# A transformer block on one core: the experts' second product in three terms, high parts of the weights by ScalarE

## The reference

```
x = layernorm(x + attention(x))                 # softmax attention, biases in all four products
xf = x.reshape(4096, 512)
ew, ei = top_k(xf @ gate_w.T, 2);  ew = softmax(ew)
expert e: (silu(xf @ w_gate[e].T) * (xf @ w_up[e].T)) @ w_down[e].T
routed = sum of the two chosen experts, each by its weight ew
shared = (silu(xf @ sh_gate.T) * (xf @ sh_up.T)) @ sh_down.T
out = layernorm(x + routed + sigmoid(xf @ se_gate_w.T) * shared)
```

## Time and profile before

| what | value |
|---|---|
| median, lowest, highest of the runs | 2044.42, 2044.05, 2047.7 us |
| the profiled execution: its own time, its span | 2047.9, 2046.2 us |
| mean granted TensorE clock | 0.989 |
| share of the chain that ended last | PE 86%, DVE 4%, DMA 3%, SPq 3%, issue 2% |
| store of the second product's result, 256 KB, issue to landing | 2.3 us, 71 of them |
| store of a high part, 256 KB | 2.4 us, 32 of them |
| load of an expert's high parts, 1 MB | 7.2 us, 8 of them |
| load of an expert's second weights, 512 KB | 20.8 us, 8 of them |

### The profile page before, as it was taken

The page is one execution under the profiler, slowest core; times in us unless marked ns, Lnnn a source line. Parts: engine busy times, 40 slices in busy tenths (PEclk is TensorE's granted clock), DMA queues, the critical chain, the costliest instruction groups (busy, mean ns, idle before and its releaser), DMA issues.

```text
span 2046.2 us, 31314 instructions
## 1 busy us (share of the span) xinstructions
PE 1971.2 (96%) x10048; PEld 1280.0 (63%) x10049; DVE 1344.6 (66%) x2296; ACT 888.2 (43%) x1571; POOL 942.9 (46%) x893
## 2 busy tenths in 40 slices
PE   7999999999999999999999998879999999999997
PEld 5655555755555755555755545568766666667886
DVE  5777776678777677777477776579233444446865
ACT  2366664366665366665266565311111111112322
POOL 3255654455665455665355556549111111114651
PEclk9999999999999999999999999989999999999999
DMA  7312433403432503432503323775643332347752
GB/s 231 73 41 70 99 79 93 140 23 85 102 79 71 162 17 82 99 92 54 170 27 69 68 74 104 260 303 181 249 170 103 102 97 98 103 168 228 224 174 71
DMA packets 103699, 242.11 MB, mean 118 GB/s; under 512 B 25296, under 2 KB 25808, under 8 KB 98576
## 3 DMA queue, kind: packets, MB, share of 16 engines
q1 hardware_dynamic: 92768, 205.06, 33.1%
q0 software_dynamic: 10800, 35.40, 6.2%
HBM read 132.93 MB, written 56.61 MB: 93 GB/s over the span
## 4 chain that ended last, share of the span: by engine, by line
PE 86%; DVE 4%; DMA 3%; SPq 3%; issue 2%; ACT 1%; POOL 1%; ACTq 0%; DVEq 0%; POOLq 0%
PE ps_gu L1698 18%; PE ps_s L723 11%; PE ps_side L701 11%; PE ps_ctx L734 10%; PE ps_side L675 9%; PE ps_d L1804 6%; PE ps_sum L747 5%; PE ps_d L1698 4%; PE ps_t L1769 1%; SPq L359 1%; PE ps_side L667 1%; DMA inv_rows<-inv_few 1%; DMA x_r<-x 1%; PE ps_side L772 1%; PE ps_side L769 1%
## 5 line engine op out<-in xcount | busy, mean ns | idle before, releaser
L1002 DVE TENSOR_REDUCE max_half<-ps_side 128x1 f32<-128x512 f32 x1024 | 658.8, 682 | 211.7 <-PE ps_side L701 208.5
L701 PE MATMUL ps_side<-kq_stack 96*128 96x512 f32 x1024 | 409.3, 404 | 4.9 <-DVE max_half L1002 2.3
L723 PE MATMUL ps_s<-kq_stack 97*128 97x512 f32 x937 | 392.2, 419 | 8.3 <-ACT probs_first L887 4.6
L723 PEld LDWEIGHTS ps_s<-kq_stack 97*128 97x128 f32 x937 | 177.4, 189 | 165.4 <-issue 85.5
L887 ACT ACTIVATE probs_first<-ps_s 128x512 f32<-128x512 f32 x326 | 187.7, 600 | 101.1 <-PE ps_s L723 85.5
L701 PEld LDWEIGHTS ps_side<-kq_stack 96*128 96x128 f32 x1024 | 195.5, 191 | 57.0 <-DVE max_half L1002 25.5
L887 ACT ACTIVATE probs_mid<-ps_s 128x512 f32<-128x512 f32 x308 | 177.5, 599 | 111.9 <-PE ps_s L723 97.3
L622 POOL TENSOR_TENSOR acc<-probs_first,probs_mid 128x512 f32<-128x512 f32 x129 | 163.8, 1296 | 131.1 <-ACT probs_mid L887 131.1
L887 ACT ACTIVATE probs_last<-ps_s 128x512 f32<-128x512 f32 x303 | 175.8, 599 | 99.2 <-PE ps_s L723 83.2
L622 POOL TENSOR_TENSOR acc<-probs_last,probs_first 128x512 f32<-128x512 f32 x129 | 163.3, 1292 | 117.6 <-ACT probs_first L887 117.6
L1653 POOL DMA_INDIRECT x_g<-x,who_all x71 | 67.4, 949 | 323.4 <-PE ps_t L1769 315.5
(11 more groups left out here) (252 smaller groups left out, 3674.2 us busy)
## 6 DMA issues: line engine op xcount, KB each, us to landing
kq_stack<-kq SPq DMA_DIRECT2D x192, 256.0 KB, 5.1
y_slots<-y_t SPq DMA_DIRECT2D x71, 256.0 KB, 2.3
x_r<-x SPq DMA_DIRECT2D x32, 256.0 KB, 3.9
x_t<-x SPq DMA_DIRECT2D x32, 256.0 KB, 4.1
gu_sb<-wgu SPq DMA_DIRECT2D x8, 1024.0 KB, 15.4
gu_kept<-gu_part SPq DMA_DIRECT2D x32, 256.0 KB, 2.4
gu_hi<-gu_kept SPq DMA_DIRECT2D x8, 1024.0 KB, 7.2
out<-gu_sb SPq DMA_DIRECT2D x32, 256.0 KB, 2.8
```

The source lines that it names most:

```text
L701: nc.tensor.matmul(bank, q_stack[par][0:3 * HD, h, t * P:(t + 1) * P], k_stack[par][0:3 * HD, h, half * HALF:(half + 1) * HALF], start=Tru ...
L723: nc.tensor.matmul(out, k_stack[par][0:3 * HD + 1, h, kt * P:(kt + 1) * P], q_stack[par][0:3 * HD + 1, h, half * HALF:(half + 1) * HALF], ...
L1002: nc.vector.reduce_max(max_half[:, u // 2, u % 2:u % 2 + 1], bank, AX.X).then_inc(side_free, 1)
```

## The change

- Attention: of the last batch's last group, the row sums of six pairs of steps (those that end no tile of keys) are issued one step later, after the second slot of scores.
- Scores: high and low router weights stand side by side (`rw_parts`), so a chunk of x takes two matmuls in place of three; what turns the scores back adds the two halves with a matrix `twice`. The first shared tile is turned and cut ahead of the last group's score (`FirstTile`).
- The high parts of the weights are made by ScalarE (`weights_high`) between its copies for the shared tiles: three parts in tile 1, five in tiles 2 to 10 each. There are now 48 parts, because the second product's weights are cut as well; their low parts (`wd_lo`) take the place of `wd_sb`, their high parts go to DRAM (`wd_kept`). GpSimd makes the low parts only, and gathers x for the first four expert tiles after part 40.
- The routing table: `positions` becomes `positions` (after tile 2) and `places` (after tile 3); all that follows comes one tile later.
- The first load of high parts is asked for when half of tile 11's product is done (`half_up`). The loads of x for shared tiles 14 and 15 move behind the expert tiles.
- Experts: x of the next tile is turned ahead of the product; two tiles are turned and cut before the pipeline. The second product has three terms: 6 fp32r matmuls, `e_hT_hi` by ScalarE, `e_hT_lo` by VectorE, `wd_hi` (512 KB a tile, two buffers) loaded by GpSimd for each tile. The last one's second product moves into the first shared product behind; the combining plan starts one tile later.

The diff, cut to its core:

```diff
@@ attention, batch(b, last)
-                            row_sums(b, loc)
+                            if not sums_later(last, loc):
+                                row_sums(b, loc)
+                        if slot == SUMS_LATER and loc and sums_later(last, loc - 1):
+                            row_sums(b, loc - 1)
@@ scores
-                    for i, (w, m) in enumerate(((rw_hi, xh), (rw_lo, xh), (rw_hi, xl))):
+                    for i, x in enumerate((xT_hi, xT_lo)):
+                        done = nc.tensor.matmul(ps_s[0:2 * RW, g, :], rw_parts[:, c].rearrange("p a n -> p (a n)"),
+                                                x[:, g, c, :], ...)
...
+                if last:
+                    first_tile.turn(pe)
@@ the table
-TABLE_AFTER = {3: (0, 1), 4: (2, 3), 5: (4, 5), 6: (6, 7)}
+TABLE_AFTER = {4: (0, 1), 5: (2, 3), 6: (4, 5), 7: (6, 7)}
@@ SyncE
-            sp.wait_ge(gu_ready, COVER)
+            sp.wait_ge(half_up, 1)
             sp.sem_inc(passed, 1)
             load_high(0)
+            sp.wait_ge(gu_ready, COVER)
             load_high(1)
...
@@ GpSimd
-            for i in range(E * C):
...
-                nc.gpsimd.tensor_copy(gu_part[:, i % 2, :], gu_sb[:, e, c, :]).then_inc(router.st_high, 1)
+            for i in range(PARTS):
+                raw, low = raw_and_low(i)
                 pool.wait_ge(router.st_high, 3 * C + i + 1)
+                nc.gpsimd.tensor_tensor(low, raw, gu_part[:, i % 2, :].bitcast(F32), ...
...
             for t in range(NT):
+                if t < 2:
...
+                else:
+                    pool.wait_ge(ey_ready, t - 1)
+                e = pool.value_load(tile_expert[0:1, t:t + 1], min_val=0, max_val=E - 1)
+                nc.gpsimd.dma_start(wd_hi[t % 2][:].bitcast(F32), wd_kept[bass.ds(e, 1)]...)
+                if t and t + 3 < NT:
+                    pool.wait_ge(et_ready, t)
+                    gather_x(t + 3)
@@ TensorE
             def expert_step(t, s):
+                if not static(t, 1) and not is_last(t):
+                    expert_turn(t + 1, (s + 1) % 4)
                 expert_up(t, s, expert_of(t))
-                if not is_last(t):
-                    expert_turn(t + 1, (s + 1) % 4)
                 if not static(t, 1):
                     expert_down(t - 1, (s - 1) % 4, expert_of(t - 1))
                 expert_turn_hidden(t, s)
@@ expert_down
+                pe.wait_ge(wd_hi_in[s % 2], wd_loads(t, s))
-                    done = nc.tensor.matmul(ps_d[:, s % 2, :], e_hT[:, s % 2, c, :], wd_sb[...], ...
+                    done = three(ps_d[:, s % 2, :], (e_hT_hi[:, s % 2, c, :], e_hT_lo[:, s % 2, c, :]),
+                                 (wd_hi[s % 2][:, c, :], low), c, CH - 1)
@@ ScalarE
+            def expert_h_high(t, s):
+                act.wait_ge(eht_ready, t + 1)
...
             def expert_step(t, s):
+                if not static(t, 1) and not is_last(t):
+                    expert_x_copy(t + 1, (s + 1) % 4)
                 expert_gate(t, s)
-                    expert_x_copy(t + 1, (s + 1) % 4)
+                expert_h_high(t, s)
...
+            def weights_high(i):
+                if i == 0:
+                    act.wait_ge(gu_in, 16 * E)
+                if i == E * C:
+                    act.wait_ge(wd_in, 16 * E)
+                if i >= 2:
+                    act.wait_ge(part_out[i % 2], 16 * (i // 2))
+                    act.wait_ge(router.st_split, 3 * C + i - 1)
+                nc.scalar.activation(gu_part[:, i % 2, :], raw_and_low(i)[0], ACT.Copy).then_inc(router.st_high, 1)
...
             for t in range(COVER):
                 gate(t)
                 if t < COVER - 1:
                     x_high(t + 1)
+                for i in itertools.islice(parts, 1 if t > 1 else 0):
+                    weights_high(i)
                 h_high(t)
                 if t == 1:
...
+                for i in itertools.islice(parts, PARTS_A_TILE - 1 if t > 1 else PARTS_FIRST * t):
+                    weights_high(i)
```

More of the change, by code:

```diff
@@ L1266, in back @@
                 for s in range(4):
-                    done = nc.tensor.transpose(ps_b[:, s, :], sT[:, g, s * P:(s + 1) * P], ident[0:RW, 0:RW])
+                    done = nc.tensor.matmul(ps_b[:, s, :], sT[:, g, s * P:(s + 1) * P], r.twice[:], start=True, stop=True)
                 done.then_inc(back_ready, 1)
@@ L1311, in group @@
                         r.low(dve, q + 1, 1 - g, s)
+                if last:
+                    first_tile.low(dve)
                 take(q, g)
@@ L1699, in three, with up @@
                 return done
-            def up(t):
+            def up(t, between=None):
                 pe.wait_ge(t_hi, t + 1)
@@ L1710, in up, with up_high_first @@
                     pe.wait_ge(ehid_done, NT)
-                    up_high_first(t)
+                    up_high_first(t, between)
                     return
-                for k in range(2):
-                    for c in range(C):
-                        done = three(ps_gu[:, k, :], (xT_hi[:, t % 2, c, :], xT_lo[:, t % 2, c, :]),
-                                     (sgu_hi[:, c, k, :], sgu_lo[:, c, k, :]), c, C - 1)
+                by_chunk = t == COVER - 1
+                for k, c in sorted(itertools.product(range(2), range(C)), key=lambda kc: kc[1] if by_chunk else kc[0]):
+                    done = three(ps_gu[:, k, :], (xT_hi[:, t % 2, c, :], xT_lo[:, t % 2, c, :]),
+                                 (sgu_hi[:, c, k, :], sgu_lo[:, c, k, :]), c, C - 1)
+                    if by_chunk and (k, c) == (1, C // 2 - 1):
+                        done.then_inc(half_up, 1)
                 done.then_inc(gu_ready, 1)
-            def up_high_first(t):
+            def up_high_first(t, between):
                 pe.wait_ge(router.st_in[0], 32)
@@ L1818, in expert_of, with step @@
                 return pe.value_load(tile_expert[0:1, bass.ds(t, 1)], min_val=0, max_val=E - 1)
-            def step(t, first, last):
-                if first:
-                    turn(t)
+            def step(t, last):
                 up(t)
@@ L1825, in step @@
                     turn(t + 1)
-                if not first:
+                if t:
                     down(t - 1)
@@ L2123, in positions, with places @@
                 link(v.tensor_tensor(big[3], big[3], cnt[4][:].unsqueeze(1).broadcast_to((P, TT, E)), ALU.add))
+                return end
+            def places(end):
+                shift = P.bit_length() - 1
                 for k in range(2):
@@ L2178, in _ @@
                 elif t == 2:
-                    positions(running)
+                    end = positions(running)
+                elif t == 3:
+                    places(end)
                 for part in TABLE_AFTER.get(t, ()):
@@ L2183, in _ @@
                     who()
+            for t in range(2):
+                expert_x_low(t, t)
             finish(COVER - 1)
-            expert_x_low(0, 0)
             expert_pipeline(dve, expert_step)
-            x_low(COVER)
             expert_y_copy(NT - 1, (NT - 1) % 4)
```

258 lines of the change are left out of this document (164 added, 94 removed).

## The result

The changed kernel takes 2072.6 us in the median of four runs (2071.18 to 2076.86), the kernel before 2044.66 (2044.05 to 2047.7, four runs). The ratio is 1.0137, 95% interval 1.0119 to 1.0155: slower by 28 us. The profiled execution took 2076.9 us, 4 above the median, with a span of 2075.2.

The account below looks back on a forecast made before the run. TensorE, busy 96% of the span, was taken as the bound, so only less PE work or closed gaps pay. The terms summed to -1 us: 2043.4 from the median 2044.42, put at 2044.5 for the clock; range 2039 to 2051, chance 0.47.

Parts of the forecast that it names:

- Start of the experts: First expert tiles: earlier turns give -5, but high-part loads slowed by competing traffic make tile 4 late, +5 (-4 to +8).
- The experts' loop: Experts' tiles: shorter second product, but the turn ahead exposes TensorE's preparation behind hid; +6 us (-23 to +20).
- its x: Experts' loop: the moved turn's share of TensorE's preparation, 0 to 0.43 us a tile, taken as 0.22.
- Rival A: Experts' loop: preparation runs ahead of the wait, array alone counts, 23 us gained; 2015.5 us, chance 0.13.
- Second weights "hidden": Experts' loop: GpSimd's 512 KB load per tile has 9 us from request to use at DMA share 0.34: hidden.
- rival D: Experts' loop: second product's high parts land late, over 9 us after request; 35 us at 10 us, 2080, chance 0.06.
- The end: After the expert tiles: last second product moves into the next tile's first product, -1 us; combining starts one tile later.
- High parts by ScalarE: Shared tiles: ScalarE waits for a store in tile 1, hidden tile 2 comes late, +7 us; later tiles +1.
- The table one tile later: Shared tiles: routing table cut in two pieces, stalls of 5.6 us in place of 9.8 and slow clock; -6 (-9.8 to 0).
- Scores and sums: Before the shared tiles: fewer score matmuls -4.5, earlier turn of tile 0 -1.8, clock -1.7, later row sums -5.
- the way of the scores back ... stays: Last score to first shared product: of 3.75 us, the scores' return, some 1.9, stays unchanged.
- Sums: Attention's last group: six row sums two scores later gain 5 us, between 2.8 and 7.5.

Follow-up runs that it names:

- parts_early: Changed kernel with ScalarE making six high parts a tile in place of five: 2075.5 us, ratio 1.0147.
- turn_to_experts: Changed kernel with shared-weight pieces ahead of part stores, the last three a step sooner, and gathers one by one behind parts 40 to 43: 2068.5 us, ratio 1.0125.
- eight_written: Changed kernel with expert tiles 0 to 7 written out, so the wait for all loads moves from tile 4 to tile 8: 2068.8 us, ratio 1.0103.
- number_early: Changed kernel with TensorE reading the next tile's expert number before the wait for hid in three of four tiles: 2058.55 us, ratio 1.0059.
- four_passes: Changed kernel with the experts' second product as two four-pass float32 matmuls from high parts alone, low parts left out: 2076.65 us, ratio 1.0148.
- hidden_inside: Changed kernel with the hidden tile turned behind the first three matmuls of the next tile's first product: 2047.2 us, ratio 1.0015.
- loads_by_sync: Changed kernel with SyncE in place of GpSimd loading the second product's high parts: 2074.6 us, ratio 1.0133.
- two_parts_first: Changed kernel with two high parts in tile 1 in place of three, six in tile 2, five in the others: 2068.85 us, ratio 1.0122.

## Why the prediction was wrong

The forecast was 2044.5 us, no change; measured were 2072.6. By its own steps:

- **Start of the experts: the step that failed.** It said of the high parts' loads: "They can't begin earlier, since they also wait for the last kept piece's landing, so asking at half a product brings nothing", and let them begin where they had begun. The piece was named and not followed: it stands in SyncE's queue behind the stores of parts, whose number had grown by half. The last part, made 30 us ahead of tile 11 before, is now made 9.0 us behind its start: 4.3 by its place in ScalarE's program, 4.7 by the gathers. Behind its store come two pieces of 1 MB. Measured: asked for 12.2 us later against the start of tile 11, and tile 11 to expert tile 4 took 15 us more, +10 over the +5 forecast. `parts_early` (asked for at 6.8 us, as before the change), `turn_to_experts` (11.0) and `eight_written` show the links. What the step did foresee, 3 us more from request to tile 4 and a wait there, was right.
- **The experts' loop: right in mechanism and size.** Forecast were pitches of 5.19 and 5.72, measured 5.11 to 5.33 and 5.73; tiles 5 to 66 took 5.3 us more, near the forecast 6, though its x was 0.10 to 0.13 in an ordinary tile and not 0.22; `number_early`, `four_passes` and `hidden_inside` show that it is TensorE's reading of the number, waits and branch behind the wait for `hid`, and not the array. Rival A was wrong for this kernel, and right for the one with the wait moved.
- **Second weights "hidden": wrong at the end of the loop.** There SyncE loads 2 MB of shared weights at a time, and the 512 KB that take 3.9 us in the median of all took 7.9 in the median of the seven issued between 1830 and 1875 us. TensorE waited at three products:

```profile
PE ps_d L1786 <- DMA wd_hi<-wd_kept: 5.2, 3, 2.5
```

  This was rival D with the right mechanism, at three products and not at all 71. That the 2 MB alone did it is not shown: in `loads_by_sync` the same loads beside the same 2 MB, asked for by SyncE ahead of them, took 5.6 us in the median of nine, and one wait of 1.2 us was left. The forecast judged by the mean DMA share of the loop, where the last tiles have a stage's change in them.
- **The end: missed.** +5.2 us, of which 2.6 are GpSimd's closing (below), 1.9 the first late shared tile, which now holds the product that moved here (1.4) and waits 0.6 for its weights, and 0.9 the third.
- **High parts by ScalarE: right in mechanism, too high in size.** Forecast: part 2 free at 1348, hidden tile 2 late by 6.5, +7. Measured: part 2 at 1352.32 after 6.63 us, TensorE idle 3.7 us, then slow clock; `two_parts_first` puts the whole at 4.
- **The table one tile later: -6 forecast, nothing came.** The wait of 9.8 us is gone as forecast, the longest is now 3.7. But TensorE's waits for `hid` up to tile 11 are 11.2 us in four and were 11.4 in three, and tiles 3 to 8 took 83.1 us and 82.5 before. The slow clock moved as well: behind the wait in tile 5 it fell on the 32 matmuls that look up the table. First before, then after:

```profile
1391.37 3.69 PE L1813 MATMUL ps_hts<-y_t,x_g 128*128 128x71 f32 x32
...
1393.86 6.94 PE L1908 MATMUL ps_hts<-y_t,x_g 128*128 128x71 f32 x32
```

  That the whole stretch from tile 0 to 11 came out near its forecast (+3.7 against +2) is luck: tiles 0 to 2 took 3.0 us more where 7 were forecast for the stall in tile 2, and this makes up for most of the 6 that the table didn't give.
- **Scores and sums: too high by half.** -8 forecast, -3.8 measured. From the first group to the seventh it took 32.0 us in place of 34.0. TensorE waits 4.1 us for router rows and not 3.1, but the larger part is a term that the prediction put at nothing ("the way of the scores back ... stays"): with `twice` that way takes eight small matmuls a group in place of four, 0.99 us in place of 0.34 (to the next turn, 1290.69 to 1291.68 and 1294.06 to 1294.40), which takes back 0.65 of the 0.92 us that four matmuls fewer give. First before, then after:

```profile
1294.06 0.41 PE L1267 MATMUL pr_b<-ident,sT 16*128 16x16 f32 x4
...
1290.69 1.06 PE L1310 MATMUL pr_b<-twice,sT 32*128 32x16 f32 x8
```

  The clock still fell at 1324: tile 0 took 9.5 us, where it took 7.9 in eight other profiles in which the clock stayed high. Sums: 5 forecast, about 3 measured.

By the stretches of the table the error from -1 to +29 us is made up so: start of the experts 10, scores and sums 7, the experts' last tiles with the slow tile 4 6, the end 5, shared tiles 2.

## What to carry to other kernels

When a change puts more items through a stage, follow the last of them through each engine's program: behind which step its copy stands, what else the next engine has to do just then, and what queues behind its store. The ring's round trip alone, 2.7 us, would not have told it here. When a product is made cheaper, count what brings its result back as well. If a loop has a gap behind a wait, less work for the busiest engine brings nothing; look first at what stands behind the wait in that engine's program, and move the wait to a place where it is long over. A wait for a whole set, placed ahead of a loop for the loop's sake, should be placed where the first member beyond the first is used.

## What the runs showed of the hardware that was not expected

- GpSimd's closing instruction (DRAIN) took 8.4 us in the fifteen profiles in which GpSimd sends 71 more DMAs, and the program ended 5.2 to 5.3 us behind SyncE's own; before, and in the two profiles in which SyncE sent these DMAs, it took 5.8 and the program ended 2.6 us behind. Whether it goes by their number or their packets (10800 before, 21024 after) wasn't tried.
- VectorE's table operations and GpSimd's subtractions slow each other: 128x1024 took VectorE 1.23 us alone and 2.19 beside a subtraction, 128x568 took 0.74 and 1.83; a subtraction took 1.3 us alone and 1.8 or more beside them (changed kernel and `parts_early`).
- A 512 KB load between two of 1 MB took 8.6 us from issue to landing (the chain of waits of the changed kernel, issued at 1869.95), over twice its median of 3.9.
- Reading the expert's number behind the wait for `hid` costs TensorE 0.36 us a tile (`number_early`), and no gap is left where 1.4 us of matmuls are queued ahead of it (`hidden_inside`).
